# Key attention of layer 0: GpSimd folds each head's 64 probabilities to 32, VectorE sums the 32

## The reference, cut to what matters

```python
def _L0_ffn_ref(x, Wq, Wk, Wv, Wo, Wff):
    q = split_heads(x @ Wq)          # 16 heads of 8 features
    k = split_heads(x @ Wk)
    v = split_heads(x @ Wv)
    scores = jnp.einsum('bqd,bkd->bkq', q, k) / jnp.sqrt(jnp.asarray(D, x.dtype))
    attn = jax.nn.softmax(scores, axis=-1)
    out = jnp.einsum('bkq,bkv->bqv', attn, v)
    z = out.reshape(B, H, S, dh).transpose(0, 2, 1, 3).reshape(B, S, L)
    z = z @ Wo
    z = _l2_normalize(z)
    z = z @ Wff
    z = _l2_normalize(z)
    return jax.nn.gelu(z, approximate=False)
```

## Time and profile before

| | before |
|---|---|
| median of 3 runs | 1991.72 us (1990.61 to 1992.4) |
| the profiled execution, its own time | 1981.9 us |
| its span | 1980.0 us |
| busy over the span: PE, DVE, ACT, POOL | 71%, 61%, 36%, 29% |
| mean granted TensorE clock | 0.813 of full speed |
| the changed stage, about 246 to 421 us | 9% of the span |

### The profile page before, as it was taken

The page is one execution under the profiler, slowest core; times in us unless marked ns, Lnnn a source line. Parts: engine busy times, 40 slices in busy tenths (PEclk is TensorE's granted clock), DMA queues, the critical chain, the costliest instruction groups (busy, mean ns, idle before and its releaser), DMA issues. The chain is left out here.

```text
span 1980.0 us, 43468 instructions
## 1 busy us (share of the span) xinstructions
PE 1402.0 (71%) x14268; PEld 1104.6 (56%) x14268; DVE 1198.5 (61%) x3390; ACT 715.2 (36%) x1769; POOL 578.3 (29%) x1087
## 2 busy tenths in 40 slices
PE   6999889848999610399939999740199656566564
PEld 3777545525777510299929999620177544454353
DVE  4888479978888650144416666550011179969896
ACT  2666456645666200122205444300033212232232
POOL 4555111112110217300066541117400187211221
PEclk9999967868999755699959999855599867677576
DMA  4222000000000001377711110001277411010001
GB/s 149 51 51 52 24 2 3 3 2 24 22 20 20 3 9 52 94 204 204 200 46 42 37 37 19 5 0 52 80 191 198 126 43 34 0 33 11 0 1 43
DMA packets 109054, 108.26 MB, mean 55 GB/s; under 512 B 12656, under 2 KB 88432, under 8 KB 108784
## 3 DMA queue, kind: packets, MB, share of 16 engines
q1 hardware_dynamic: 100720, 89.61, 16.6%
q0 software_dynamic: 8192, 16.79, 3.0%
HBM read 81.19 MB, written 25.17 MB: 54 GB/s over the span
## 5 line engine op out<-in xcount | busy, mean ns | idle before, releaser
L2220 DVE COPY e_xT<-e_pX 128x256 f32<-128x256 f32 x72 | 30.5, 424 | 318.9 <-PE e_pX L2281 318.9
L2281 PE MATMUL e_pX<-W,e_rows 128*128 128x128 f32 x144 | 28.9, 284 | 213.5 <-DMA e_rows<-slots_in 212.3
L2292 PE MATMUL e_H<-e_xT,e_w_up 128*128 128x256 f32 x736 | 175.3, 386 | 1.2 <-DMA e_w_up<-in_f_dram 1.2
L2292 PEld LDWEIGHTS e_H<-e_xT,e_w_up 128*128 128x128 f32 x736 | 137.3, 194 | 18.2 <-DVE e_xT L2220 1.6
L2281 PEld LDWEIGHTS e_pX<-W,e_rows 128*128 128x128 f32 x144 | 18.6, 147 | 216.1 <-DMA e_rows<-slots_in 215.7
L2302 PE MATMUL e_pY<-e_w_down,e_h 128*128 128x128 f32 x992 | 125.9, 279 | 15.1 <-ACT e_h L2269 13.8
L2302 PEld LDWEIGHTS e_pY<-e_w_down,e_h 128*128 128x128 f32 x992 | 120.8, 193 | 27.7 <-issue 19.5
L2141 POOL DMA_INDIRECT slots_in<-R,r_put x96 | 92.0, 958 | 57.1 <-issue 29.0
L428 DVE TENSOR_REDUCE a_mx<-a_S 128x8 f32<-128x1024 f32 x64 | 78.1, 1220 | 32.0 <-PE a_S L513 31.8
L473 ACT ACTIVATE a_PT<-a_ST 128x1024 f32<-128x1024 f32 x64 | 65.5, 1024 | 79.1 <-PE a_ST L540 79.1
L2258 ACT ACTIVATE e_silu<-e_H 128x256 f32<-128x256 f32 x120 | 46.0, 383 | 124.1 <-PE e_H L2292 124.1
(11 more groups left out here) (415 smaller groups left out, 4202.5 us busy)
## 6 DMA issues: line engine op xcount, KB each, us to landing
e_w_up<-in_f_dram SPq DMA_DIRECT2D x40, 384.0 KB, 3.6
e_w_down<-in_f_dram SPq DMA_DIRECT2D x32, 322.0 KB, 3.1
e_rows<-slots_in SPq DMA_DIRECT2D x72, 128.0 KB, 3.0
slots_out<-e_y SPq DMA_DIRECT2D x72, 128.0 KB, 3.5
e_w_up<-in_f_dram SPq DMA_DIRECT2D x32, 256.0 KB, 3.7
e_w_down<-in_f_dram SPq DMA_DIRECT2D x40, 192.0 KB, 3.2
slots_in<-Y SPq DMA_DIRECT2D x32, 160.0 KB, 2.5
a_cK<-in_ctxT_dram SPq DMA_DIRECT2D x64, 64.0 KB, 1.8
```

Of the source, the lines that this page charges most:

```text
L2292: i = nc.tensor.matmul(H[:, banks * p + b, CHUNK * c:CHUNK * (c + 1)], up[:, p, at:at + P], xT[:, p, :], start=True, stop=True)
```

## The change

GpSimd adds, for each head, the first 32 and the last 32 probabilities of tile t-7 into a new tile `half` (128 x 16 x 32, two buffers), ahead of its two small instructions of the step. VectorE sums the 32 that are left of each head, from `half`, and this `divide_v` has moved from lag 7 to lag 8.

```diff
+        half = sb("half", [P, 2, HEADS, T // 2])
...
-            pipeline(pool, NT, [(1, lambda u, p: ln.pool_rstd(pool, u, p))],
+            def add_halves(u, p):
+                done(pool, s_exp, u)
+                free(pool, s_sum, u)
+                nc.gpsimd.tensor_tensor(half[:, p], Pr[:, u % DEPTH, :, 0:T // 2], Pr[:, u % DEPTH, :, T // 2:],
+                                        ALU.add).then_inc(s_half, 1)
+
+            pipeline(pool, NT, [(7, add_halves), (1, lambda u, p: ln.pool_rstd(pool, u, p))],
                      straight=True)
...
-                    free(dve, s_sum, u, bufs=DEPTH)
+                    free(dve, s_half, u, bufs=DEPTH)
...
             def divide_v(u, p):
-                done(dve, s_exp, u)
+                done(dve, s_half, u)
                 free(dve, s_rd, u)
-                nc.vector.tensor_reduce(sums[:, p, :], Pr[:, u % DEPTH], AX, ALU.add).then_inc(s_sum, 1)
+                nc.vector.tensor_reduce(sums[:, p, :], half[:, p], AX, ALU.add).then_inc(s_sum, 1)
...
-                               (0, lambda u, p: ln.vector_stats(dve, u, p)), (7, divide_v)], straight=True)
+                               (0, lambda u, p: ln.vector_stats(dve, u, p)), (8, divide_v)], straight=True)
```

More of the change, by code:

```diff
@@ L599, in key_attention0_stage @@
         s_xt, s_xts, s_proj, s_qkv = sem("xt"), sem("xt_out"), sem("proj"), sem("qkv")
-        s_spread = sem("spread")
+        s_spread, s_half = sem("spread"), sem("half_sums")
         s_S, s_mx, s_sub, s_exp, s_sum = sem("scores"), sem("max"), sem("sub"), sem("exp"), sem("sum")
```

## The result

| | before | after |
|---|---|---|
| median over all its runs | 1984.71 us (1974.46 to 1992.40, 13 runs) | 1996.03 us (1990.97 to 1999.67, 13 runs) |
| ratio to before | | 1.0059 (95% interval 1.0042 to 1.0077) |
| profiled execution: span, mean granted clock | 1980.0 us, 0.813 | 1995.5 us, 0.802 |

The change makes the kernel slower: by the ratio, 11.7 us of 1984.71 (8.3 to 15.3). The forecast was 9.8 us, 1.0049. The absolute times moved with more runs (before was 1991.72 in its first three and 1984.71 over thirteen), so the ratio is the number to compare. The 2001.5 us of the forecast stood on the first three runs; on the median of thirteen it would be 1984.7 + 9.8 = 1994.5, against 1996.03 measured.

A forecast was written before the change was run, and what follows sets the result against it. VectorE was taken to set the pace at 4.90 us a step, with stalls where TensorE fell behind at half clock. 9.8 - 1.9 - 0.45 + 1.0 + 1.35 = +9.8 on the median 1991.72 gave 2001.5 us, range 1987 to 2012.

The forecast's parts named there:

- Where it falls: GpSimd's add occupies 320.82 to 322.09 in every step; V's multiplication (321.04) and the normalisation (321.25) start inside it.
- E: The end of a step's second subtraction on VectorE, 319.86 us in the profile before; steps are counted from it.
- How long the hold outlasts the add: V's multiplication, held by GpSimd's add, ends some 0.15 us after it; the normalisation took 0.09.
- The step: VectorE's step in the changed stage grows by 0.39 us, from 4.90 to 5.29.
- Rival 1: Not slower: the add holds only the normalisation, not V's multiplication; step 0.07 longer, -0.9 in all, 1991 us; chance 0.13.
- Rival 2: Clearly faster: nothing held, V starts before the add; TensorE sets some 4.6 us a step; -12.7, 1979 us; chance 0.11.
- rival 3: Much slower: TensorE's clock stays at the lower level, each of 25 steps takes 6.07 us; some 2018 us; chance 0.06.
- stage start to the end of step 8's subtraction: Step 7 loses its division; VectorE alone would gain up to 1.73 us, TensorE holds most back: -0.45.
- the 25 steps after it, stalls included: Steps 8 to 32, with add, V and normalisation in order: 25 x 0.39 = +9.8, less 1.9 of stalls.
- steps 33 to 35: Steps without normalisation and statistics go from 4.38 to 4.72 us: 3 x 0.33 = +1.0.
- last subtraction to the last V: Four divisions left at the end instead of three, two held by adds; 4.93 becomes 6.28 us: +1.35.
- the stalls: VectorE's stalls, 2.9 us over 25 steps, shrink as TensorE has 0.39 us more a tile: -1.9, between 0 and -2.9.

The follow-up runs named there:

- the kernel with its reciprocals in PSUM: Changed kernel with the reciprocals in PSUM instead of SBUF, so V's multiplication has one SBUF input; 1.0038 of before.
- the add of one column: Changed kernel with GpSimd's add on one column of 512, waits and order kept, result not right; 0.9910 of before.
- the add after the maximum at lag 7: Changed kernel with GpSimd's add waiting for the first maximum of tile u+2, and the division back at lag 7; 0.9905 of before.
- the other two kernels: Changed kernel with the add on one column of 512, 0.9910 of before; changed kernel with the add waiting for the first maximum, division at lag 8, 0.9912.
- the add alone: Kernel before with GpSimd's add of the halves put in, its result unused, VectorE still summing 1024 columns at lag 7; 1.0046 of before.
- The add in two: Changed kernel with the add as two instructions of 256 columns (heads 0 to 7, 8 to 15), same place, no new wait; 1.0018 of before.

## Why the prediction was right

The mechanism came as it was put, and it was not only argued: the multiplication is held until 0.15 us after the add, and each of its conditions was switched by a run of its own.

- The sum over 512 columns: 0.68 expected, 0.67 measured.
- The add: 1.27 expected, 1.26 measured. The slope between the 128- and 256-column adds gave 1.29, near it; the line to the 1,892 ns of the square, which reads one tile twice, gave 1.12.
- Where it falls: 0.96 after E expected, 338.36 - 337.37 = 0.99 measured. That the two engines hang on the same moments and so meet in every step was right.
- How long the hold outlasts the add: 0.15 expected, 0.15 measured. No row had this number for an instruction with two SBUF inputs; the rows had 0.09, for L241. That it came out so exactly was luck.
- The step: 5.29 expected, 5.31 measured.

The choice that carried the forecast was to class the multiplication with L241, which the earlier trace rows show held, and not with L442, which is not. Rival 1, the other choice, is real, but for the kernel with its reciprocals in PSUM. Rival 2's condition, VectorE ahead of the add, did not occur, and rival 3's, TensorE at half clock for good, neither.

The sum in its terms, between the same events in both profiled executions. The stage is counted from the end of tile 0's second subtraction (260.92 before, 262.61 after) to the last V's start (418.22 and 432.79), and the 25 steps run from 274.71 to 400.12 and from 276.94 to 411.98:

| term | predicted | measured |
|---|---|---|
| stage start to the end of step 8's subtraction | -0.45 | +0.5 |
| the 25 steps after it, stalls included | 9.8 - 1.9 = +7.9 | 135.0 - 125.4 = +9.6 |
| steps 33 to 35 | +1.0 | +1.2 |
| last subtraction to the last V | +1.35 | 6.42 - 4.93 = +1.5 |
| stage | +9.8 | +12.9 |

Two terms were mis-sized. The first is the start. The prediction let the adds cost something only from step 8 on, where a division stands in front of L241. But steps 6 and 7 have adds too (of tiles 0 and 1), and L241 itself waits for L234, which ends 0.04 us after the add has started, so the add held it, twice:

```profile
268.14 1.22 DVE L241 TENSOR_SCALAR f_xn<-X,f_ln_moments,f_ln_rstd 128x128 f32<-128x128 f32 x1 [0.81 <-issue]
```

```profile
267.50 0.55 POOL L234 TENSOR_TENSOR f_ln_rstd<-f_ln_rstd,f_ln_half 128x1 f32<-128x1 f32 x1
268.01 1.26 POOL L621 TENSOR_TENSOR f_half<-f_Pr 128x512 f32<-128x512 f32 x1
```

That is 1.22 instead of 0.34 us in two steps, and it ate what step 7 saved: with the add of one column that step is 4.45 us instead of 4.90, the expected -0.45, and with the full add 4.94. The second is the stalls: I took 1.9 of 2.9 us off for a slower VectorE that TensorE can catch up with. 135.0 less 25 x 5.31 are 2.3, so only 0.6 went. Steps of 5.79, 6.06 and 6.07 us stand near 300 us, where TensorE was busy 39 of 40 us from 276 to 316, at half clock for the first 20 and at a mean of 0.67 after.

```profile
276.00:296.00 20.00, 19.83 (x279) 11.53 (x275) 19.48 (x39) 11.83 (x31) 7.99 (x12) 0.50 0.01 2
296.00:316.00 20.00, 19.02 (x353) 11.08 (x353) 17.81 (x34) 12.68 (x42) 6.00 (x9) 0.67 0.01 2
```

The rest between the profiled executions (15.5 us of span against 12.9 in the stage) is 1.7 us in which the stage before ended later, and 0.9 behind it, neither of which the change touches. By the ratio of all runs the change costs 11.7 us and not 15.5; the profiled execution before took 1981.9 us, less than its median of 1984.71. So the term of the stalls, which differ between executions of one kernel, is the least certain of the table.

## What to carry to other kernels

Before work goes to GpSimd, ask what VectorE reads while GpSimd runs, not only whether GpSimd has time: at 2.1 of 5 us it had plenty, and the kernel still lost 0.6%. In these traces a VectorE multiplication with two SBUF inputs, or a tensor_scalar from SBUF to SBUF, ended only after a GpSimd add that started ahead of it, and showed the wait as its own duration; the ones that take a tile from PSUM ran beside it. So time the GpSimd instruction, with a wait if need be, to lie beside VectorE's PSUM reads: here one semaphore wait turned 1.0059 into 0.9912.

## What the runs showed of the hardware that I had not expected

Rival 2 took 4.6 us a step for a TensorE that goes to and fro between its two clock levels. The three kernels with a step of 4.37 came near that mean by another way. With the add after the maximum at lag 7, the subtractions that open and close the 25 steps are these:

```profile
270.77 0.69 DVE L640 TENSOR_TENSOR f_Pr<-f_S,f_mx 128x512 f32<-128x512 f32 x1
...
384.97 0.69 DVE L640 TENSOR_TENSOR f_Pr<-f_S,f_mx 128x512 f32<-128x512 f32 x1
```

They are 114.2 us apart, 4.57 a step, against 125.4 before (the other two kernels: 115.1 and 116.8). The steps above 4.37 lie together at the start, up to 6.07 us long, with TensorE at half clock; after them the granted clock stayed at the upper level, 2.4 GHz, to the end of the stage's middle. Stretches of the same trace (columns as in the earlier trace rows):

```profile
276.00:296.00 20.00, 20.00 (x281) 11.95 (x281) 15.53 (x37) 11.45 (x33) 7.03 (x12) 0.51 0.01 2
296.00:316.00 20.00, 17.78 (x445) 10.92 (x444) 18.73 (x45) 15.89 (x55) 9.06 (x13) 1.00 0.01 3
316.00:336.00 20.00, 16.77 (x429) 10.17 (x431) 19.35 (x47) 15.92 (x51) 8.87 (x15) 1.00 0.01 2
336.00:356.00 20.00, 16.88 (x405) 10.34 (x390) 19.41 (x46) 14.90 (x51) 9.66 (x15) 1.00 0.02 5
```

From 296 to 396 us it is 1.00 there, with TensorE busy 16.5 to 17.8 of 20 us, and in the other two from 316 to 396. The kernel before, at a step of 4.90, had 0.74 and 0.91, and the add alone, at 5.27, between 0.67 and 0.98 from 296 us on. A step of 5.18 had one such stretch too: the add in two, 1.00 from 356 to 376 us. Over all runs the mean granted clock of the whole execution was between 0.814 and 0.818 in the median for the three kernels, and 0.803 and 0.806 for the kernel before in its two sets of runs.

So a TensorE at full clock, which lets VectorE wait less, may be a part of what the well-placed add gains, but the profiles do not show it: what the 25 steps took above 25 x 4.37 is 5.0 to 7.6 us in these kernels, and above 25 x 4.90 it was 2.9 before. The profiled executions also differ by only 12.0 us (1980.0 - 1968.0) where the ratio at lag 7 makes 18.8. What moved the clock, no run varied by itself; it stays open, and so does the rest of the gain.
